# A graph-attention layer on one core: x's normalisation moved to ScalarE, GpSimd's steps respread, transposes put between the halves of a score

## The reference

```python
h = jnp.maximum(_layernorm(x, axis=-1), 0.0)
neib_att = jnp.tanh(neigh @ Wn1 + bn1) @ Wn2 + bn2      # D_HID = 32
value = neigh @ Wv + bv                                 # D_OUT = 128
x_att = jnp.tanh(h @ Wx1 + bx1) @ Wx2 + bx2
ws = leaky_relu(x_att @ neib_att.T, 0.01)               # 4096 x 4096
ws = softmax(where(adj > 0, ws, -9e15), axis=1)
out = x + concatenate([h @ Wfx + bfx, ws @ value], axis=1)
```

## Time and profile before

| | |
|---|---|
| median of 3 executions | 519.95 us (519.1 to 520.16) |
| the profiled execution | 519.84 us, span 518.0 us |
| TensorE busy | 480.9 us (93%) |
| VectorE busy | 451.8 us (87%) |
| ScalarE busy | 417.6 us (81%) |
| GpSimd busy | 210.0 us (41%) |
| mean granted TensorE clock | 0.988 |

### The profile page before, as it was taken

One profiled execution on the slowest core, in us unless ns is written; L12 is line 12 of the kernel. 1 busy time (PEld: TensorE's weight loads), 2 busy tenths in 40 slices (PEclk: granted clock), 3 DMA queues, 4 the chain that ended last, 5 costly groups with the idle time before them and its releaser, 6 DMA issues.

```text
span 518.0 us, 8865 instructions
## 1 busy us (share of the span) xinstructions
PE 480.9 (93%) x2812; PEld 374.6 (72%) x2855; DVE 451.8 (87%) x883; ACT 417.6 (81%) x585; POOL 210.0 (41%) x324
## 2 busy tenths in 40 slices
PE   5697978799999999999999999999999999998996
PEld 4365667587778778777878777877777787766884
DVE  1679878989999899989998999899999989985664
ACT  2562797899889988998889888988899889997552
POOL 1503113145644564446544664366336444530100
PEclk9997998999999999999999999999999999999999
DMA  6864774565456544664567445744565555500100
GB/s 180 217 203 79 142 137 79 113 112 94 81 92 139 116 76 85 127 144 81 82 127 156 77 75 105 159 80 80 110 135 82 82 95 118 90 5 1 42 0 22
DMA packets 38530, 52.07 MB, mean 101 GB/s; under 512 B 4436, under 2 KB 30292, under 8 KB 38484
## 3 DMA queue, kind: packets, MB, share of 16 engines
q0 software_dynamic: 9216, 33.56, 39.3%
q1 hardware_dynamic: 29268, 17.95, 11.7%
HBM read 80.86 MB, written 4.19 MB: 164 GB/s over the span
## 4 chain that ended last, share of the span: by engine, by line
PE 55%; ACT 17%; issue 9%; POOL 7%; DVE 7%; DMA 4%; SPq 1%; DVEq 0%; ACTq 0%; POOLq 0%
PE ps_turned L904 14%; PE ps_scores L881 9%; ACT scores L515 7%; PE ps_product L925 7%; PE ps_product L923 7%; PE ps_product L924 6%; POOL scores L409 5%; ACT scores L503 5%; ACT pt_hi L479 4%; PE ps_scores L880 4%; PE ps_product L849 3%; DMA scores<-in_L_gnn_neigh 3%; DVE mask L645 2%; DVE pt_lo L658 1%; PE ps_product L787 1%
## 5 line engine op out<-in xcount | busy, mean ns | idle before, releaser
L658 DVE TENSOR_TENSOR pt_lo<-ps_turned,pt_hi 128x512 fp32r<-128x512 f32 x256 | 173.4, 684 | 34.3 <-ACT pt_hi L479 19.1
L479 ACT ACTIVATE pt_hi<-ps_turned 128x512 fp32r<-128x512 f32 x256 | 155.4, 608 | 56.5 <-PE ps_turned L904 56.2
L409 POOL TENSOR_TENSOR scores<-scores,mask 128x512 f32<-128x512 f32 x109 | 126.7, 1162 | 176.7 <-ACT scores L503 176.6
L904 PE MATMUL ps_turned<-ident,scores 128*128 128x128 f32 x1024 | 154.7, 274 | 3.6 <-DVE pt_lo L658 3.1
L904 PEld LDWEIGHTS ps_turned<-ident,scores 128*128 128x128 f32 x1024 | 124.1, 140 | 45.5 <-DVE pt_lo L658 17.2
L503 ACT ACTIVATE scores<-ps_scores 128x1024 f32<-128x1024 f32 x128 | 132.0, 1031 | 13.3 <-PE ps_scores L881 13.3
L515 ACT ACTIVATE scores<-scores,neg_top 128x2048 f32<-128x2048 f32 x64 | 129.0, 2015 | 0.0
L676 DVE CUSTOM_DVE_ANT_0 scores<-ps_scores,scores,top 128x1024 f32<-128x1024 f32 x96 | 122.5, 1276 | 3.2 <-ACT scores L503 2.7
L923 PE MATMUL ps_product<-pt_hi,v_hi 128*128 128x512 f32 x256 | 122.0, 477 | 0.2 <-DVE pt_lo L658 0.2
L881 PE MATMUL ps_scores<-neib,xs 128*128 128x512 f32 x256 | 109.9, 507 | 6.0 <-DVE top L676 2.9
L925 PE MATMUL ps_product<-pt_lo,v_hi 128*128 128x512 f32 x256 | 101.4, 396 | 0.0
(11 more groups left out here) (75 smaller groups left out, 378.1 us busy)
## 6 DMA issues: line engine op xcount, KB each, us to landing
adj_in<-in_adj POOLq DMA_DIRECT2D x64, 512.0 KB, 5.4
scores<-in_L_gnn_neigh SPq DMA_DIRECT2D x8, 512.0 KB, 5.5
x_rows<-in_x SPq DMA_DIRECT2D x8, 512.0 KB, 5.4
x_left<-in_x SPq DMA_DIRECT2D x8, 256.0 KB, 3.0
x_right<-in_x SPq DMA_DIRECT2D x8, 256.0 KB, 2.8
out_h<-x_left SPq DMA_DIRECT2D x8, 256.0 KB, 4.2
out_h<-x_right SPq DMA_DIRECT2D x8, 256.0 KB, 3.4
scores<-in_x SPq DMA_DIRECT2D x1, 512.0 KB, 4.0
```

The lines of the kernel that those rows point to most:

```text
L409: pool.tensor_tensor(half, half, mask[:, s % MASK_RING, BANK:CHUNK], ALU.add).then_inc(masked, 1)
L479: act.activation(pt_hi[:, (2 * b + u) % HI_RING], pt[:, u], ACT.Copy).then_inc(hi_done, 1)
L658: dve.tensor_tensor(pt_lo[:, u], pt[:, u], pt_hi[:, (2 * b + u) % HI_RING].bitcast(FP32), ALU.subtract).then_inc(lo_done, 1)
L904: last = pe.transpose(pt[:, u, i * P:(i + 1) * P], scores[:, parity * TILES + i, n * P:(n + 1) * P], ident[:, :])
```

## The change

1. **ScalarE normalises x.** Relu(x * rstd + shift) with shift = -mean * rstd, from two small operations added to GpSimd's series. The copies of the transposed x drop their relu. ScalarE also writes the high part of x's stack, as Identity with a bias; VectorE keeps the low part.
2. **Stages in other steps.** The table gives x's stages new steps: load 8 to 6, statistics 9, 10, 11, 12 to 10, 10, 11, 12, aggregation 13 to 12, Newton 13, 13, 14, 15 to 14, 14, 15, 15, normalisation 1, 1, 3, 3 to 0, 2, 4, 4, first layer 8 to 9, second layer 12, 13 to 13, 13, left half 15 to 18 to 15, 16, 18, 19 with its end from 18 to 19.
3. **GpSimd's sums**: x_left's 9, 10 to 8, 18; x_right's from 10, 11 of a group to 12, 13. One in a step.
4. **TensorE** runs the first four transposes of a step between the score's halves.
5. **VectorE** closes a group before it negates the maximum.

```diff
-X_LOAD, X_STATS, X_AGGR = -8, -7, -3
-X_RSTD = (-3, -3, -2, -1)
-X_NORM = (1, 1, 3, 3)
-X_TURN = 6
-X_FIRST = 8
-X_TANH = 11
-X_SECOND = 12
-X_STACK = 13
-X_WIDE, X_LEFT = 15, 18
-X_LEFT_LOAD, X_SUM = 4, 9
-X_RIGHT = 6
+X_LOAD = -10
+X_STATS = (-6, -6, -5, -4)
+X_AGGR = -4
+X_RSTD = (-2, -2, -1, -1)
+X_NORM = (0, 2, 4, 4)
+X_TURN = (6, 7)
+X_FIRST, X_TANH = 9, 11
+X_SECOND = (13, 13)
+X_STACK = (13, 14)
+X_WIDE, X_LEFT = (15, 16, 18, 19), 19
+X_LEFT_LOAD, X_SUM = 4, (8, 18)
+X_RIGHT = 8
...
-NEWTON_OPS = 2 + 4 * NEWTON
+NEWTON_OPS = 4 + 4 * NEWTON
...
+        mean_neg = sb("mean_neg", [P, TILES], FP32)
         rstd = sb("rstd", [P, TILES], FP32)
+        shift = sb("shift", [P, TILES], FP32)
...
                     pool.tensor_scalar(var_eps[:, :], mean_var[:, :, 1], EPS, None, ALU.add).then_inc(newton, 1)
-                    pool.wait_ge(newton, done + 1)
+                    pool.tensor_scalar(mean_neg[:, :], mean_var[:, :, 0], -1.0, None, ALU.mult).then_inc(newton, 1)
+                    pool.wait_ge(newton, done + 2)
...
                     pool.tensor_tensor(rstd[:, :], rstd[:, :], factor[:, :], ALU.mult).then_inc(newton, 1)
+                    if i == NEWTON:
+                        pool.wait_ge(newton, done + 4)
+                        pool.tensor_tensor(shift[:, :], mean_neg[:, :], rstd[:, :], ALU.mult).then_inc(newton, 1)
...
+            def x_stack_high(e, par, bank):
+                if e == 0:
+                    act.wait_ge(b2_in, B2_IN)
+                act.wait_ge(x_second, e + 1)
+                wait(act, scored, GSTEPS * (e - 1))
+                act.activation(xs[:, par, :], bank, ACT.Identity, bias=b2[:, 1:2]).then_inc(x_att_hi, 1)
+
             def neigh_step(e):
                 q = e
                 par = e % 2
+                if e == NEIGH_GROUPS - 1:
+                    x_stack_high(0, 0, x_bank(0))
                 if e == NEIGH_GROUPS - 2:
                     x_tanh(0, x_bank(0))
+                if e == 1:
+                    for i in range(TILES):
+                        x_normalise(0, i)
...
+            def x_normalise(e, i):
+                act.wait_ge(x_rows_in, 16 * (e + 1))
+                act.wait_ge(newton, NEWTON_OPS * (e + 1))
+                act.activation(x_rows[:, i, :], x_rows[:, i, :], ACT.Relu, bias=shift[:, i:i + 1],
+                               scale=rstd[:, i:i + 1]).then_inc(x_normed, 1)
+
             def x_turned_copy(e, k, bank):
...
-                act.activation(x_rows_t[:, k, :], bank, ACT.Relu).then_inc(x_turned_out, 1)
+                act.activation(x_rows_t[:, k, :], bank, ACT.Copy).then_inc(x_turned_out, 1)
...
+                for i in range(TILES):
+                    if e := x_due(s, X_NORM[i]):
+                        x_normalise(e, i)
                 for k in range(KT):
-                    if e := x_due(s, X_TURN + k):
+                    if e := x_due(s, X_TURN[k]):
                         x_turned_copy(e, k, x_bank(e))
                 if e := x_due(s, X_TANH):
                     x_tanh(e, x_bank(e))
+                if e := x_due(s, X_STACK[0]):
+                    x_stack_high(e, e % 2, x_bank(e))
...
-            def x_normalise(e, i):
-                dve.wait_ge(x_rows_in, 16 * (e + 1))
-                dve.wait_ge(newton, NEWTON_OPS * (e + 1))
-                dve.tensor_scalar(x_rows[:, i, :], x_rows[:, i, :], mean_var[:, i, 0:1],
-                                  rstd[:, i:i + 1], ALU.subtract, ALU.mult).then_inc(x_normed, 1)
-
-            def x_stack_high(e, par, bank):
-                dve.wait_ge(x_second, e + 1)
-                wait(dve, scored, GSTEPS * (e - 1))
-                dve.tensor_scalar(xs[:, par, :], bank, b2[:, 1:2], None, ALU.add).then_inc(x_att_hi, 1)
...
                 lo(s, 0)
+                close(s)
                 negate(s)
-                close(s)
                 x_work(s)
...
             def step(s):
                 score(s, 0)
+                turn(s, 0)
                 score(s, 1)
-                turn(s, 0)
                 product(s, -2)
                 turn(s, 1)
```

More of the change, by code:

```diff
@@ L369, in rstd_of @@
                 else:
-                    done = done + 2 + 4 * (i - 1)
+                    done = done + 3 + 4 * (i - 1)
                     pool.wait_ge(newton, done)
@@ L414, in step @@
                 for i in range(2):
-                    if e := x_due(s, X_SUM + i):
+                    if e := x_due(s, X_SUM[i]):
                         left_sum(e, i)
@@ L575, in neigh_step @@
                 if e == 1:
-                    for i in range(TILES):
-                        x_normalise(0, i)
                     x_aggr(1)
                 if e == NEIGH_GROUPS - 1:
-                    x_stack_high(0, 0, x_bank(0))
                     x_stack_low(0, 0, x_bank(0))
@@ L698, in x_work @@
                 for i in range(TILES):
-                    if e := x_due(s, X_STATS + i):
+                    if e := x_due(s, X_STATS[i]):
                         x_stats(e, i)
-                    if e := x_due(s, X_NORM[i]):
-                        x_normalise(e, i)
                 if e := x_due(s, X_AGGR):
                     x_aggr(e)
-                if e := x_due(s, X_STACK):
-                    x_stack_high(e, e % 2, x_bank(e))
-                if e := x_due(s, X_STACK + 1):
+                if e := x_due(s, X_STACK[1]):
                     x_stack_low(e, e % 2, x_bank(e))
@@ L943, in side @@
                 for i in range(2):
-                    if e := x_due(s, X_TURN + i):
+                    if e := x_due(s, X_TURN[i]):
                         x_turn(e, i, x_bank(e))
-                    if e := x_due(s, X_SECOND + i):
+                    if e := x_due(s, X_SECOND[i]):
                         x_second_layer(e, i, x_bank(e))
@@ L950, in side @@
                 for i in range(TILES):
-                    if e := x_due(s, X_WIDE + i):
+                    if e := x_due(s, X_WIDE[i]):
                         x_wide_layer(e, [i], x_bank(e))
```

## The result

Four runs of the changed kernel took 514.02 to 515.66 us, median 514.92, where four of the kernel before had a median of 519.99 on the same chip: the ratio is 0.990, with a 95% interval of 0.989 to 0.992. The change makes the kernel 1.0% faster. The forecast was 507.2 us, with a range of 502.0 to 514.5: the sign was right, the time lies just above the range, and the gain of 5.1 us is under half of the 12.7 that were forecast. The profiled execution took 515.66 us, span 513.9.

A forecast was written before the change was run, and what follows sets the result against it. VectorE at its limit and a four-step loop bound the kernel. Savings of 0.8 before step 0, 1.0 and 1.5 to step 31, 8.5 over five groups, 0.9 at the end: 12.7, median 507.2 us, range 502 to 514.5.

The forecast's parts named there:

- TensorE's own work: In a group of 16 steps, TensorE has 51.2 us of work it cannot avoid and 3.2 us of stalls.
- GpSimd's inverse square roots: Series moved to steps 14, 14, 15, 15: adds of steps 15 and 0 late by 1.4 and 1.5 us, 0.7 charged a group.
- ScalarE's wait for the roots: In step 0 the first normalisation waits for the last Newton round, ending about 0.5 us late, within the 0.7 charged.
- ScalarE's prices: Normalisation 0.56 us (bounds 0.38 and 0.69), less 0.1 overlap, and stack part 0.6: 2.4 us more on ScalarE a group.
- it fits, barely: One GpSimd sum to a step: add, DMA issue and sum end after 2.5 us, when the next add is due.
- The order on TensorE: Transposes between the score's halves: each loop of four steps loses 0.23 us, the last 15 steps 0.9 us.
- The term of 0.8: Before step 0, ScalarE writes the stack part while VectorE still works on the row before: 0.8 us saved.
- Same work: TensorE's side work moves off even steps, leaving the loops where ScalarE waits; no gain was entered for it.
- The third, ScalarE as the bound: ScalarE becomes the bound: 53.9 us a group, 513.2 us in all; chance 0.22.
- The second, TensorE alone: TensorE alone sets the pace, GpSimd's lateness is absorbed: 51.6 us a group, 501.7 us in all; chance 0.16.
- The fourth: The score's second half comes too late for odd steps' rises: gain gone at 0.2 us excess, 523 at 0.25; chance 0.09.
- the fifth: The loop of four steps holds each group where it is, VectorE's relief turns idle: 519.5 to 520.5 us; chance 0.05.

The follow-up runs named there:

- a_roots_back: The changed kernel with GpSimd's Newton series back in its old steps 13, 13, 14, 15 (one line undone); 508.34 us, ratio 0.978.
- a_norm_later: The changed kernel, Newton series still late, with the first normalisation in step 2 instead of 0; 513.69 us, ratio 0.989.
- a_roots_norm_odd: The changed kernel with the Newton series back in its old steps and ScalarE's normalisations in steps 1, 1, 3, 3; 514.56 us, ratio 0.990.
- c_odd_steps_stack_dve: The changed kernel with GpSimd's extra work all in odd steps and the high part of x's stack back on VectorE; 512.93 us, ratio 0.988.

## Why the prediction was off

**The bound.** *VectorE runs at its own limit, and its relief is worth something*: right. The normalisations are worth 0.93 us a group, the stack part 0.65, the order 0.34; together 1.9, near the 1.6 us by which the group falls from 54.4 to 52.80 when nothing else gets in the way.

**TensorE's own work: too low.** The first failed step. The forecast gave TensorE 51.2 us of work it cannot avoid, and so 3.2 us of stalls to win back. In a_roots_back the chain is nothing but TensorE and adds up to 52.8. The difference by the pieces of that chain: the second layer is 0.89 us for its 8 matmuls and not 0.45 (+0.45; in the kernel before each of its halves, at 241.26 for one, took the 0.45 that the forecast gave to both); scores are 11.2 us and not 10.9 (+0.3); transposed blocks 14.8 and not 14.1, since some first blocks behind a score take 0.56 instead of 0.44 (+0.7); products 22.25 and not 22.1 (+0.2). The clean pieces of the earlier trace rows were multiplied as if every piece were clean. So only 1.6 us a group were to be won, and the whole change without the late series wins all of it. The forecast for this case was 52.0 (52.7 less the 0.7 for the roots): 0.8 too low, five times over 4 us of the 7.7 missing.

**GpSimd's inverse square roots: the mechanism right, the size wrong.** The second failed step. Foreseen were adds 1.4 and 1.5 us late; they came 1.5 us late, both. Foreseen was a leak with 0.3 us to give; the free part is 0.3 to 0.5 us. The step that fails is the discount: "TensorE has some 0.5 us of side work less in step 1 to catch up with, so I charge 0.7". A score that waits for a leak isn't helped by a shorter queue before it, least of all on the engine that is the bound. 1.36 us a group were paid, 0.66 more than charged, 3.3 us over five groups. With the 4 us above that is 7.3 of the 7.7 that the medians lack. (The profiled execution lacks 8.6: 7.2 in the groups, 1.6 in the first 32 steps, less 0.3 that the tail gained.)

**ScalarE's wait for the roots** was 1.2 us and not 0.5. "More than 1 us" stood among the signs of a wrong forecast, and rightly; but the wait is a symptom, and its removal bought nothing in the group (a_norm_later).

**ScalarE's prices**: right. The normalisation takes 0.63 us and the stack part 0.68, both within the bounds of 0.38 and 0.69; that is 0.07 more than the 0.56 taken for the first, but two normalisations in a row start about 0.5 us apart, and the sum of 2.4 us came out.

```profile
L475 ACT ACTIVATE x_rows<-x_rows,shift,rstd 128x256 f32<-128x256 f32 x4 | 2.4, 630 | 1.2 <-POOL shift L387 1.2
...
L447 ACT ACTIVATE xs<-ps_product,b 128x512 fp32r<-128x512 f32 x1 | 0.7, 677 | 0.0
```

That even steps hide them was right and is worth 6 us (a_roots_norm_odd). The 0.4 charged for the pair in step 4 was not there.

**GpSimd's sums**: "it fits, barely" was right, and so was what was left unsaid: with the masks at 1.13 us hidden anyway, it brought nothing.

**The order on TensorE**: the effect is there, the reason isn't. The forecast was 0.23 us in each loop of four steps, 0.9 in the last 15. Undoing the order there costs 0.18 us (47.39 to 47.57), and the order alone gives the kernel before 0.49 (48.22 to 47.73). The first transposes no longer wait for the score's second half, but they wait for VectorE's low part of the step before, which follows on the same leak that the score waited for. These are the waits in the last 15 steps of before, then of after:

```profile
PEld ps_turned L904 <- DVE pt_lo L658: 0.7, 2, 0.4
```

```profile
PEld ps_turned L916 <- DVE pt_lo L674: 2.2, 8, 0.3
```

The 0.83 us that the last 15 steps did gain agree with the forecast 0.9 by accident: the rest is there with the old order too (48.22 to 47.57), and no run took it apart further; side work of TensorE moved between steps there as well, and VectorE closes a group before it negates.

**The first 32 steps.** Forecast were 3.3 us up to the rise of step 32, and the profiled execution has 1.7 (141.70 to 139.96). That is a sum of terms that were each wrong. Steps 16 to 31, "like a full group", were to give 1.5 and gave 0.14; with the series early they still took 50.65. Up to step 0 the changed kernel was three microseconds later (48.36 against 45.28) and not 0.8 earlier. The clock has a part in it: up to step 0 TensorE's mean granted clock was 0.86 there and 1.00 before, while the step after it ran at 0.50 before (6.68 us) and at 1.00 in the changed kernel (3.94). The term of 0.8 can't be read from two such starts.

Steps 0 to 15 were to give 1.0 and gave 4.7. Part of it is that first step, but 4.0 us lie in two others, after the rises of steps 8 and 12. Before, then after, in the columns of the earlier trace rows:

```profile
68.69:71.57 2.88, 2.69 (x30) 2.15 (x31) 1.61 (x4) 1.66 (x4) 1.32 (x2) 1.00 0.83 181
78.99:83.36 4.37, 4.18 (x18) 3.58 (x19) 2.75 (x11) 1.65 (x3) 0.80 (x4) 0.61 0.13 26
```

```profile
70.73:72.36 1.63, 1.30 (x10) 0.54 (x12) 1.22 (x5) 1.56 (x3) 0.27 (x1) 1.00 0.75 251
79.89:81.51 1.62, 1.12 (x7) 0.82 (x7) 1.41 (x9) 1.51 (x4) 0.00 (x0) 1.00 0.75 149
```

In the kernel before, TensorE stands 0.92 us there for ScalarE's copy ahead of the first layer, and 0.98 us for the tanh ahead of the second; behind the latter its granted clock falls to 0.50 for a part of the stretch (0.61 over all of it). The changed kernel has the first layer in step 9 and the whole second one in step 13. All four traced kernels with the old table of stages have these long steps, with 45.5 to 46.0 us for steps 0 to 15; all thirteen with the new one, as it is or slightly altered, have neither (at most 2.09 and 1.62 us), and 39.7 to 42.3 us, also with the normalisations or the stack part back on VectorE. So most of the 5.1 us was gained in the first group, and by the waits it comes from where TensorE's side work stands, the term that the prediction put at nothing ("Same work"). No run moved that work alone: the place of the gain is shown, the stage that makes it is argued. That the forecast was no further off is luck.

**The rivals.** The third, ScalarE as the bound with 53.9 us a group and 513.2 in all, came nearest in numbers (54.17, 514.9) and is not what happened: with the same work on ScalarE the group is 52.80 once the series is early. The second, TensorE alone, is what happens without the late series, at 52.8 instead of 51.6. The fourth did not occur: no rise waits for a score in the group. Nor did the fifth, as a group of 52.80 us shows. The 0.8 us for ScalarE's stretches and small meetings, which the forecast added to TensorE's 51.2, were not there; TensorE's own pieces took their place.

VectorE's rows decided against the advice weighed in the prediction: four relus with scale and bias are 4.2 us better off on ScalarE here, though each is longer there (0.63 against 0.42 us). The Trainium skill, "Perfetto Trace Analysis", section "Optimizing Scalar/DVE Operations", has the condition that was missing: if VectorE is saturated, offloading some of its work to ScalarE may make sense. The runs agree, with 53.73 us a group one way and 52.80 the other.

## What to carry to other kernels

Before the gain of a relieved engine is forecast, add up the bounding engine's pieces over a whole period, not the clean pieces times their number: what is left above that sum is all that can be won. When a helper engine has its work in a short slot, moving another operation may shorten the slot; check every engine's due times after all moves together, and charge what lies beyond the slack in full if it reaches the engine that is the bound. And the place of moved work in a period can be worth as much as the move: here 6 us hung on odd or even steps, and 6.6 on one step earlier. Look at the first period by itself: there the bounds are others, and here it held most of the gain.

## What the hardware showed that was not expected

A mask on VectorE, bf16 to bf16, 0.41 us by itself, took 3.00 us in one place (341.75) and 2.98 in another kernel (342.81), while GpSimd had a sum, an add and a sum without gaps. It began 0.17 and 0.15 us before the first of them, during GpSimd's DMA issue, and ended 0.3 us after the last. A third one, of 2.50 us, stood in the same way behind a sum and an add. The Trainium skill, "SBUF — State Buffer", section "SBUF: two separate sides", says of VectorE's operations in a two-port mode that whichever of the two engines starts first gets the shared port pair for its whole instruction, and that the other blocks. By that one would expect a wait for at most one operation; here, by the recorded starts, it lasted through three. No run shows which mode this mask had, nor whether the issue counts as the first start. In the run where the sums stood apart from the next add (c_odd_steps_stack_dve) no mask passed 1.01 us.

Small operations on GpSimd differ in how they chain: most of 128 x 4 elements took 0.19 to 0.23 us, and two dependent steps of the series mostly start 0.27 to 0.42 us apart, but seven chained memsets of that size took 1.05 us together, 0.15 each.
